# Layer 0's one-hots made by eight Abs and a Relu on ACT instead of a comparison on DVE, and other source rows for empty slots

## The reference, cut to what matters

```python
row, col = (edge_index[0], edge_index[1])          # src, dst
h = jnp.tanh(scaled[:, None] @ Wf1 + bf1)
filters = (h @ Wf2 + bf2) * cut[:, None]
fsum = jnp.sum(filters, axis=-1, keepdims=True)
messages = x[col] * fsum                           # gather by destination
agg = jax.ops.segment_sum(messages, row, num_segments=x.shape[0])
out = jax.nn.softplus(agg @ Wi1 + bi1) @ Wi2 + bi2
```

## Time and profile before

| | us |
|---|---|
| median of 3 runs (7854.47 to 7868.76) | 7855.23 |
| profiled execution | 7849.15 |
| its span | 7847.1 |
| POOL busy, of the span | 5484.3 |
| DVE busy | 3031.3 |
| ACT busy | 1682.6 |
| layer 0's pass by destination, first scatter to last | 1521.96 to 2694.35 |

### The profile page before, as it was taken

How to read it: one execution, slowest core, us unless ns; L and a number is a source line. 1 busy time by engine, 2 the same in 40 slices (tenths; PEclk the granted TensorE clock), 3 DMA queues, 4 the chain that set the end, 5 groups by cost and what they waited for, 6 DMA issues and landing times. The chain is left out here.

```text
span 7847.1 us, 86403 instructions
## 1 busy us (share of the span) xinstructions
PE 3358.7 (43%) x17325; PEld 2980.5 (38%) x17326; DVE 3031.3 (39%) x9623; ACT 1682.6 (21%) x4060; POOL 5484.3 (70%) x5252
## 2 busy tenths in 40 slices
PE   3100000144444485444442444443777775444443
PEld 1000000144444474444442444442666664444443
DVE  9888201122222365222225222225232235444444
ACT  3100000111111384222222222223222223100000
POOL 2688777777777773777774777773777771777775
PEclk9555555566666697555555655555777777556656
DMA  6132333344444462444443444443444442444444
GB/s 216 47 88 76 90 100 91 113 143 142 143 141 144 138 212 60 132 131 133 130 132 51 132 130 133 130 133 61 136 135 136 133 135 14 131 131 131 130 131 95
DMA packets 519984, 943.40 MB, mean 120 GB/s; under 512 B 221340, under 2 KB 257668, under 8 KB 519784
## 3 DMA queue, kind: packets, MB, share of 16 engines
q1 hardware_dynamic: 348392, 637.41, 24.3%
q0 software_dynamic: 171520, 305.19, 18.2%
HBM read 673.90 MB, written 270.82 MB: 120 GB/s over the span
## 5 line engine op out<-in xcount | busy, mean ns | idle before, releaser
L1323 POOL DMA_INDIRECT edge_buf<-node_table,ixr x1664 | 1610.6, 968 | 584.4 <-issue 506.5
L1323 POOL DMA_INDIRECT Y<-node_table,ixr x1664 | 1584.6, 952 | 507.1 <-issue 507.1
L409 POOL DMA_INDIRECT edge_records<-edge_buf x800 | 990.0, 1238 | 252.6 <-issue 248.1
L1231 POOL DMA_INDIRECT layer_messages<-edge_buf,ixr x832 | 908.5, 1092 | 285.2 <-issue 263.3
L1053 PE MATMUL bank<-edge_buf,Y 128*128 128x129 f32 (+2 forms) x3744 | 818.8, 405 | 215.0 <-ACT edge_buf L1467 105.9
L1481 PE MATMUL bank<-adc,turned_buf 128*128 x2496 | 341.0, 193 | 1299.9 <-DVE z L1439 855.5
L1053 PE MATMUL bank<-Y 128*128 128x129 f32 (+1 forms) x3328 | 766.8, 421 | 248.6 <-ACT Y L1467 130.5
L1053 PEld LDWEIGHTS bank<-edge_buf,Y 128*128 128x128 f32 x3744 | 757.7, 306 | 243.7 <-issue 120.1
L1433 DVE TENSOR_REDUCE pk<-bank 128x16 f32<-128x48 f32 (+1 forms) x312 | 101.3, 325 | 1882.1 <-DMA edge_buf<-node_table,ixr 952.0
L1053 PEld LDWEIGHTS bank<-Y 128*128 128x128 f32 x3328 | 712.3, 322 | 272.2 <-issue 219.8
L1481 PEld LDWEIGHTS bank<-adc,turned_buf 128*128 128x128 bf16 x2496 | 256.1, 103 | 1442.2 <-issue 1386.6
(11 more groups left out here) (276 smaller groups left out, 5175.7 us busy)
## 6 DMA issues: line engine op xcount, KB each, us to landing
Y<-onehots SPq DMA_DIRECT2D x416, 512.0 KB, 3.8
turned_buf<-onehots_turned SPq DMA_DIRECT2D x312, 256.0 KB
edge_buf<-edge_records SPq DMA_DIRECT2D x208, 288.0 KB
layer_messages<-ACC SPq DMA_DIRECT2D x26, 2112.0 KB
onehots<-Y SPq DMA_DIRECT2D x104, 512.0 KB, 2.7
XI<-layer_messages SPq DMA_DIRECT2D x78, 528.0 KB, 3.6
edge_records<-H SPq DMA_DIRECT2D x1, 29952.0 KB
onehots_turned<-turned_buf SPq DMA_DIRECT2D x104, 256.0 KB
```

The lines of the kernel that those rows point to most:

```text
L409: pool.indirect_dma_start(rec_d, bass.IndirectOffsetOnAxis(ap=ixs[h][:, j:j + 1], axis=0), rec[h][:, j, :], None).then_inc(scattered[h], 16)
L1231: pool.indirect_dma_start(msg_d, bass.IndirectOffsetOnAxis(ap=ixr[h][:, j:j + 1], axis=0), rows[h][:, j, 0:MW], None, bounds_check=SLOTS - ...
L1323: pool.indirect_dma_start(ring[q][:, j, 0:w], None, table, bass.IndirectOffsetOnAxis(ap=ixr[q][:, j:j + 1], axis=0)).then_inc(rows_in[q], 16)
```

## The change

Two edits. In setup, the padding record's source row is set by an iota to p*8 + j for slot j of partition p (0 to 1023) instead of 0; the rest of the record stays. In layer 0's pass by destination, the comparison leaves DVE's `prepare`, with its waits. ACT makes the one-hot as relu(1 - |location - column|): eight Abs over 128 columns each, with the location as bias column (its address is computed from the half's number), then one Relu over all 1024. ACT's order is now make_onehot(0), then for each n: make_onehot(n+1), copy_turned(n). ACT waits for `kept`, `pe_done` and `oh_out` before the first Abs, and for its own last Abs before the Relu.

```diff
                         st.then(pool.memset(pr[:, :, R_POS:R_POS + 1], float(SKIP)))
+                        st.then(pool.iota(pr[:, :, R_SRC:R_SRC + 1], [[1, G], [1, 1]], base=0, channel_multiplier=G,
+                                          allow_small_or_imprecise_dtypes=True))
...
-        def onehot(h, loc):
-            return nc.vector.tensor_tensor(tiles_of_half(oh[h]), iota_row[:, :].unsqueeze(1).to_broadcast([P, G, P]),
-                                           loc.to_broadcast([P, G, P]), ALU.is_equal)
...
                         dve.wait_ge(kept[h], i + 1)
-                        if later(i):
-                            dve.wait_ge(pe_done, i * 2 + h - 1)
-                            dve.wait_ge(oh_out[h], i * 16)
-                        onehot(h, fields[:, bass.ds(t, G), 0:1]).then_inc(oh_ready, 1)
...
+                    def make_onehot(i, h):
+                        act.wait_ge(kept[h], i + 1)
+                        if later(i):
+                            act.wait_ge(pe_done, i * 2 + h - 1)
+                            act.wait_ge(oh_out[h], i * 16)
+                        for j in range(G):
+                            ins = nc.scalar.activation(oh[h][:, j * P:j * P + P], iota_row[:, :], ACT.Abs, scale=-1.0,
+                                                       bias=dlocs[:, bass.ds(((i * 2 + h) * G + j) * 5, 1)])
+                        ins.then_inc(distance, 1)
+                        act.wait_ge(distance, i * 2 + h + 1)
+                        nc.scalar.activation(oh[h], oh[h], ACT.Relu, bias=one1[:, :], scale=-1.0).then_inc(oh_ready, 1)
...
-                    looped(act, ITERS, lambda i, first: [copy_turned(i, h) for h in range(2)])
+                    act.wait_ge(ones_set, 1)
+                    make_onehot(0, 0)
+                    def body(i, last):
+                        for h in range(2):
+                            nh, step = ahead(h)
+                            if not (last and h == 1):
+                                make_onehot(i + step, nh)
+                            copy_turned(i, h)
+                    body(0, False)
+                    with act.Fori(1, ITERS - 1) as i:
+                        body(i, False)
+                    body(ITERS - 1, True)
```

More of the change, by code:

```diff
@@ L1077, in layer0_dst_pass @@
                 sem(n) for n in ("oh_ready", "pe_done", "ohT_ready", "narrowed", "psum_free"))
-            cleared = sem("cleared")
-            fields = XI[:, :, :].rearrange("p b f -> p (b f)")[:, 0:NT * 5].rearrange("p (t k) -> p t k", k=5)
+            cleared, ones_set, distance = sem("cleared"), sem("ones_set"), sem("distance")
+            dlocs = XI[:, :, :].rearrange("p b f -> p (b f)")[:, 0:NT * 5]
+            fields = dlocs.rearrange("p (t k) -> p t k", k=5)
             rec_v = rec_d.rearrange("(k p j) w -> k p (j w)", p=P, j=G)
@@ L1147, in _ @@
                         nc.vector.memset(rows[h][:, :, D:D + 8], 0.0).then_inc(cleared, 1)
-                    nc.vector.memset(one1[:, :], 1.0)
+                    nc.vector.memset(one1[:, :], 1.0).then_inc(ones_set, 1)
                     dve.wait_ge(cleared, 2)
```

## The result

The changed kernel takes 8017.08 us (median of 4 runs, 8011.91 to 8027.78), the kernel before 7856.05 beside it: ratio 1.0204, 95% interval 1.0187 to 1.022. It is 161 us slower; 150 were forecast, to a median of 8005. The profiled execution took 8027.78, the highest of its four runs, with a span of 8025.8. It is 178.6 us longer than the profiled execution of the kernel before, more than the 161 between the medians, because that one stood 6.9 us under its median and this one 10.7 above.

A forecast was written before the change was run, and what follows sets the result against it. POOL's scatters were taken to bound layer 0's destination pass, until a 13.0 us loop through DVE, ACT and PE replaced them. 7849.15 + 190 (pass) - 40 (gathers) = 7999, so a median of 8005; range 7923 to 8097.

The forecast's parts named there:

- a ring of 13.0 us: Layer 0's destination pass: DVE, ACT and PE wait on each other in a loop, 13.0 us a half, +191 us.
- POOL's pace: Layer 0's destination pass: eight scatters a half set the time, 11.15 us before, 10.2 us undisturbed.
- the pass's ends: Layer 0's destination pass: first multiplication 7.0 us later, last multiplication to last scatter's end 7.8 us shorter; pass +190.
- turn to pick: From the start of PE's turn to the start of its pick of a half: 1.75 us.
- the pick: PE's matmuls that pick for a half, before DVE's multiplication: 3.1 us, from rows of 3.09, 2.62 and 3.62.
- upper bound of 4.0: Eight Abs on ACT with nothing overlapped: 8 x (0.40 + 0.10) = 4.0 us, against 2.55 taken.
- The gathers: Ends of four later passes: different source rows for empty slots save 10 us a pass, 40 in all.
- a lag of 3.6 us: End of a gather pass: DVE's last half follows POOL's last gather by 3.6 us, instead of 13.7.
- The 1.0 us a half charged to the comparison: Layer 0's destination pass: DVE's one-hot comparison lengthens POOL's scatters by about 1.0 us a half.
- ring of 13.8 us: Upper edge of the forecast's case, a loop between 12.2 and 13.8 us a half, chance 0.82.
- The ring never fell under POOL's pace: Rival for layer 0's destination pass: the loop stays under 10.2 us a half, giving 7717 us; chance 0.08.
- ACT's register instructions: Much slower rival: they are not hidden behind activations and all picks take 3.62 us, giving 8211 us; chance 0.07.

The follow-up runs named there:

- copies_first: The changed kernel with ACT's order turned round, so that the turned copies of a half stand ahead of making the next one-hot: 7767.15 us, ratio 0.9895 to the kernel before.
- early_fields: The changed kernel with DVE keeping the five fields of half n+2 before it finishes half n, not after: 7729.37 us, ratio 0.9849 to the kernel before.
- abs_halved: The changed kernel with each Abs of 128 columns cut into two of 64, sixteen instead of eight: 8134.38 us, ratio 1.0362 to the kernel before.

## Why the prediction was right, point by point

*The mechanism.* It forecast a ring of 13.0 us that replaces POOL's pace. The changed kernel's multiplications run from 1527.84 to 2878.51, 13.11 a half. The last turn is a short one (see the pass's ends); the 102 before it take (2874.94 - 1527.84) / 102 = 13.21 each. Cutting the ring at either of two places (`copies_first`, `early_fields`) gave back more than the change had lost.

*The terms of the ring.* In the turn shown above, predicted against measured: multiplication to fields 1.80, 1.67; fields to first Abs 0.50, 0.48; Abs 2.55, 2.48 to the Relu's start; Relu 1.15, 1.15; copies 1.95, 1.93 from the Relu's end (2008.12) to 2010.05; to the turn 0.14, 0.05; turn to pick 1.75, 1.77; the pick 3.1, 3.52; to the multiplication 0.04, 0.14. The eight Abs take 2.44 us, which is the lower bound, the time of the activations with fixed addresses in the earlier trace rows; the computed addresses cost nothing. For the upper bound of 4.0 the 0.10 us added to each came from no row.

*The term that was off* is the pick. I had taken 3.1 out of a spread of 2.6 to 3.6. The groups before and after (count, busy us, mean ns):

```profile
L1191 PE MATMUL bank<-H,Y 128*128 x1664 | 330.9, 382 | 3.7 <-DVEq L1144 3.7
...
L1185 PE MATMUL bank<-H,Y 128*128 x1664 | 351.8, 400 | 1.5 <-DVEq L1138 1.5
```

That is 3.18 us a pick before and 3.38 after, 0.28 more than the term. The cause is TensorE's clock. Two picks of the changed kernel (start and end, length; busy us of PE and PEld; granted clock, DMA share, GB/s):

```profile
2819.84:2823.46 3.62, 3.57 (x16) 3.27 (x16) 0.50 0.85 280
2876.43:2878.48 2.05, 2.04 (x16) 1.85 (x16) 1.00 0.25 93
```

The same sixteen matmuls take 3.62 us at a granted clock of 0.50 (1.2 GHz) and 2.05 at 1.00 (2.4 GHz); picks of other lengths lie between, as one of 3.09 us at a mean of 0.61. Stretches of some 100 halves of the pass, in the order before, after, `copies_first` (busy us by engine; then granted clock, DMA share, GB/s):

```profile
1530.00:2650.00 1120.00, 494.04 (x2400) 472.38 (x2400) 310.26 (x601) 205.31 (x400) 866.24 (x798) 0.65 0.43 143
```

```profile
1540.00:2860.00 1320.00, 514.25 (x2395) 489.13 (x2395) 180.81 (x500) 552.58 (x1300) 777.88 (x801) 0.63 0.36 121
```

```profile
1530.00:2620.00 1090.00, 472.21 (x2420) 451.99 (x2421) 182.22 (x504) 569.00 (x1312) 782.42 (x806) 0.66 0.43 149
```

For nearly the same number of matmuls PE was busy for 494, 514 and 472 us, less where the granted clock was higher. With rings of 11.15, 13.1, 10.7 and 14.3 us (`abs_halved`) the mean matmul of the pick was 382, 400, 361 and 371 ns. That is no rule by length, and no run here shows beforehand which ring meets the high clock where.

*The pass's ends.* The start was right: the first multiplication 8.1 us later, of which 1.5 had been lost in setup already, so 6.6 for 7.0. The end was wrong in its parts. The timeline of DVE:

```profile
2874.94 1.29 DVE L1133 TENSOR_TENSOR edge_buf<-bank,XI 128x512 f32<-128x512 f32 x2 [10.85 <-PE bank L1185]
...
2878.51 1.29 DVE L1133 TENSOR_TENSOR edge_buf<-bank,XI 128x512 f32<-128x512 f32 x2 [1.88 <-PE bank L1185]
```

The last half needs no further one-hot, so its multiplication comes 3.57 us after the one before, not 13; POOL then does have a half in arrears, and needs 25.6 us to its last scatter, not 18.2. I had counted the last turn in full (9.4 too much) and the arrears not at all (7.4 too little). In sum POOL's last scatter of the pass ends at 2904.15 instead of 2694.35, 210 us later against the 190 forecast: 1 more at the start, 21 from turns of 13.21 instead of 13.0, 9 less in the last turn, 7 more after it.

*The gathers.* Forecast -40, measured -51 alone, and within the change the same (212 without the new rows, 161 with them). I had let a lag of 3.6 us stand; it is 1.54. The mechanism was only half of what I wrote: not that a gather reads one row 128 times, but that all gathers in a row read the same one.

*How near the number came.* 161 against 150 is nearer than its parts: the pass lost 20 us more than forecast and the gathers gave back 11 more. That the two errors are of opposite sign is luck. Two readings were loose besides. The 1.0 us a half charged to the comparison came from a mean that also holds the scatter of 7.41 us; the 92 us given back are 0.9 a half. And the ring of 13.8 us named as the forecast's upper edge is reached by no sum in it: picks of 3.62 make 13.5.

*The rivals.* The ring never fell under POOL's pace, and ACT's register instructions did stay hidden (eight Abs in 2.44 us). The inference of the Trainium skill ("SBUF — State Buffer", Who interferes with whom) that a tensor_tensor leaves descriptor generation alone does not hold for these scatters: they take 1.91 us beside one long comparison, 1.05 and 1.11 beside short ones, and 0.97 beside comparisons that read one SBUF tensor. The scatters also read their indices from SBUF, and the same section of "SBUF — State Buffer" in the Trainium skill says that a second SBUF input does contend with a GpSimd instruction that reads SBUF; that sentence fits all runs. It does not account for the scatter that one cast of a single input lengthened.

## What to carry to other kernels

Before moving work to an idle engine, write down the ring through that engine's queue, with its other work in it: ACT was 21% busy, and the move cost 212 us because the one-hot came to stand ahead of four copies that PE needed, and behind a copy that DVE made late. If the move is right, the order must move with it: keeping the fields one half earlier turned the whole change from 161 us slower into 118 faster. And if what was wanted is only to free POOL, change the form of the instruction on DVE first; here that gave 89 us by itself and, with the new source rows, the fastest kernel.

## What the runs showed of the hardware

- An indirect DMA on POOL is lengthened by a DVE comparison with two SBUF inputs beside it: by 0.94 us beside one of 1.23 us, and by 0.2 us a half beside eight short ones. How much depends on what is left of the DVE instruction: the scatter at 2018.68 came when 1.07 us were left and grew by 0.94; the one at 2671.63 came when 6.57 us of an addition were left and grew by 6.44. Both grew by the rest less 0.13 us.
- Eight comparisons of one SBUF tensor with a column, 1.82 us together, left the scatters' mean at 982 ns, that of the changed kernel, where DVE makes none. A cast of one SBUF tensor, 128x832, did lengthen the scatter beside it, by 0.43 us.
- Gathers in which every descriptor names one row of a table in HBM take some 12.6 ns a read (12.9 us for 1024), slower than POOL issues them; with eight rows in turn the lag is 2.6 us, with 128 rows 1.5.
- An Abs of 64 columns costs four fifths of one of 128: sixteen in 3.92 us, eight in 2.44.
- The same sixteen matmuls of a pick take 3.62 us at a granted clock of 0.50 and 2.05 at 1.00.
